# The conditional stage's fetches on SyncE in another order: expert numbers and weights one tile ahead

## What is computed

```
x = x + attn(cond(x, itok_8))
x = x + ffn(cond2(x, itok_15))

def cond2(x, indices):                       # the part that matters here
    h = gelu(x @ fc1_w.T + fc1_b)            # 256 -> 1024
    shared = h @ fc2_w.T + fc2_b             # 1024 -> 192
    expert_x = h @ experts_w[indices].T + experts_b[indices]   # 1024 -> 64, one of 16 experts per sequence
    return concatenate([shared, expert_x])
```

## Time and profile before

| | us |
|---|---|
| median of 3 runs | 1197.22 (1196.6 to 1199.02) |
| the profiled execution | 1193.99 |
| its span, first to last instruction | 1192.2 |
| phase 2 in it, from the first fc1 matmul to the first matmul of phase 3 | 391.16 to 601.24 |
| PE busy over the span | 1126.9 (95%) |

### The profile page before, as it was taken

The page is one execution under the profiler, slowest core; times in us unless marked ns, Lnnn a source line. Parts: engine busy times, 40 slices in busy tenths (PEclk is TensorE's granted clock), DMA queues, the critical chain, the costliest instruction groups (busy, mean ns, idle before and its releaser), DMA issues.

```text
span 1192.2 us, 18922 instructions
## 1 busy us (share of the span) xinstructions
PE 1126.9 (95%) x6178; PEld 898.6 (75%) x6178; DVE 803.2 (67%) x1440; ACT 594.3 (50%) x989; POOL 218.9 (18%) x266
## 2 busy tenths in 40 slices
PE   4899999999997899999699999999999999999998
PEld 3567777777764688878588888888888888888886
DVE  2776767767765655656448886588755887658775
ACT  1356556555564334433246555465554565555653
POOL 2243333433434243345100000000000000000000
PEclk9999999999999999999899999999999999999999
DMA  3341111221131446553623453134431344313430
GB/s 101 117 149 55 50 60 54 62 61 50 60 142 55 169 156 218 200 175 114 238 71 103 147 170 130 53 123 142 158 124 53 123 142 165 116 53 121 150 99 36
DMA packets 66763, 135.96 MB, mean 114 GB/s; under 512 B 13792, under 2 KB 28016, under 8 KB 66544
## 3 DMA queue, kind: packets, MB, share of 16 engines
q1 hardware_dynamic: 57696, 114.49, 29.4%
q10 hardware_dynamic: 9024, 20.97, 4.9%
HBM read 107.65 MB, written 30.41 MB: 116 GB/s over the span
## 4 chain that ended last, share of the span: by engine, by line
PE 75%; DVE 7%; SPq 6%; DMA 4%; POOL 4%; issue 3%; ACT 1%; DVEq 0%; POOLq 0%; ACTq 0%
PE bank L1459 34%; PE bank L1421 10%; PE bank L1471 5%; PE bank L1398 4%; PE bank L1209 3%; SPq L361 3%; PE bank L1190 3%; DVE neg_max L849 2%; PE bank L1267 2%; PE bank L1230 2%; PE bank L1193 2%; PE bank L1172 2%; DMA exp_raw<-in_exp_w 2%; POOL fc2b_lo L543 2%; PE bank L1156 2%
## 5 line engine op out<-in xcount | busy, mean ns | idle before, releaser
L1459 PE MATMUL bank<-op_lo,w_ring 128*128 128x512 f32 x896 | 348.6, 389 | 0.0
L1459 PE MATMUL bank<-op_hi,w_ring 128*128 128x512 f32 x896 | 348.6, 389 | 0.0
L1024 DVE TENSOR_TENSOR op_lo<-x_blk,op_hi 128x512 fp32r<-128x512 f32 x288 | 193.8, 684 | 30.4 <-ACT op_hi L722 30.3
L722 ACT ACTIVATE op_hi<-x_blk 128x512 fp32r<-128x512 f32 x288 | 162.8, 620 | 73.6 <-PE bank L1459 69.3
L1459 PEld LDWEIGHTS bank<-op_hi,w_ring 128*128 128x128 f32 x896 | 168.2, 188 | 34.9
L1459 PEld LDWEIGHTS bank<-op_lo,w_ring 128*128 128x128 f32 x896 | 168.2, 188 | 34.9
L849 DVE TENSOR_REDUCE neg_max<-bank 128x2 f32<-128x512 f32 (+1 forms) x192 | 126.0, 685 | 53.4 <-PE bank L1193 52.5
L576 ACT ACTIVATE p<-bank 128x512 f32<-128x512 f32 x192 | 111.2, 598 | 68.7 <-PE bank L1209 65.0
L746 ACT ACTIVATE x_blk<-x_blk,scales 128x512 f32<-128x512 f32 x96 | 69.3, 722 | 67.0 <-DVE x_blk L1077 28.9
L1421 PE MATMUL bank<-tile_hi,ffn_w 128*128 128x512 f32 x256 | 101.5, 396 | 0.0
L1421 PE MATMUL bank<-tile_lo,ffn_w 128*128 128x512 f32 x256 | 101.5, 396 | 0.0
(11 more groups left out here) (128 smaller groups left out, 1949.2 us busy)
## 6 DMA issues: line engine op xcount, KB each, us to landing
w_ring<-hid_scratch SPq DMA_DIRECT2D x112, 512.0 KB, 4.6
hid_scratch<-comb ACTq DMA_DIRECT2D x8, 1792.0 KB, 6.7
comb<-in_hid_d ACTq DMA_DIRECT2D x6, 768.0 KB, 4.6
xt<-in_x_t SPq DMA_DIRECT2D x16, 256.0 KB
xtok<-in_x_tok SPq DMA_DIRECT2D x16, 256.0 KB
resid<-in_x_t SPq DMA_DIRECT2D x16, 256.0 KB, 3.1
x_scratch<-x SPq DMA_DIRECT2D x16, 256.0 KB, 2.6
tile_in<-x_scratch SPq DMA_DIRECT2D x8, 512.0 KB, 4.2
```

The source lines that it names most:

```text
L722: nc.scalar.activation(op_hi[:, o % OP_RING, k], x_blk[:, operand_home(o), k], ACT.Copy).then_inc(s["op_hi"], 1)
L1024: nc.vector.tensor_tensor(op_lo[:, o % OP_RING, k], x_blk[:, operand_home(o), k], op_hi[:, o % OP_RING, k].bitcast(F32), ALU.subtract).the ...
L1459: last = mm(banks[first_bank + m][:, :], w, read(v[:, q % OP_RING, k, :]), start=k == 0 and v is op_hi and i not in (P2, P3), stop=k == KB ...
```

## The change

SP's program of the stage is written out for all tiles instead of looped, and put in another order. `load_expert` is divided: `expert_ids(t)` loads both numbers, `load_expert(t, ids)` issues both weight DMAs behind `expert_split` alone, and `load_expert_bias(t, ids)` issues both bias DMAs behind `y_ready`. In the round of tile t SP issues the input of tile t+1, the numbers and weights of t+1, the store of y of t, and the biases of t+1. The `w_ring` loads come behind everything that tile 7 needs, `load_y(1)` now stands ahead of the last store of `y`, and DVE has one added wait on `y_stored` in phase 3.

```diff
-            def load_expert(t):
-                for j in range(BT):
-                    e = sp.value_load(expert[0:1, bass.ds(t * BT + j, 1)], min_val=0, max_val=E - 1)
+            def expert_ids(t):
+                return [sp.value_load(expert[0:1, t * BT + j:t * BT + j + 1], min_val=0, max_val=E - 1) for j in range(BT)]
+
+            def load_expert(t, ids):
+                if t:
+                    sp.wait_ge(s["expert_split"], HEAD + BT * t)
+                for j, e in enumerate(ids):
                     sp.dma_start(exp_raw[:, j], exp_w[bass.ds(e, 1)].rearrange("a p k h -> p (a k) h")).then_inc(s["expert_loaded"], 16)
+
+            def load_expert_bias(t, ids):
+                if t:
+                    sp.wait_ge(s["y_ready"], HEAD + (1 + BT) * t)
+                    settle(sp, "sp_settled")
+                for j, e in enumerate(ids):
                     sp.dma_start(fc2_bias[SHARED - P:P, 1 + j:2 + j], exp_b[bass.ds(e, 1)].rearrange("a p o -> p (a o)")).then_inc(s["bias_loaded"], 16)
 
+            ids = expert_ids(0)
+            load_expert(0, ids)
             sp.dma_start(fc2_bias[:, 0:1], fc2_b[0]).then_inc(s["bias_loaded"], 16)
...
+            load_expert_bias(0, ids)
...
-            def cond2_tile(t, more):
-                if not is_first(t):
-                    sp.wait_ge(s["expert_split"], HEAD + BT * t)
-                    sp.wait_ge(s["y_ready"], HEAD + (1 + BT) * t)
-                    settle(sp, "sp_settled")
-                load_expert(t)
-                if more:
-                    load_x(t + 1)
-                else:
-                    sp.wait_ge(s["xa_split"], HEAD + TILES)
-                    sp.wait_ge(s["y_stored"], HEAD + 16)
-                    sp.dma_start(yc[:, :, :], y_scratch[:, :, 0:TW]).then_inc(s["yc_loaded"], 16)
+            def store_y(t):
                 sp.wait_ge(s["y_ready"], HEAD + (1 + BT) * (t + 1))
...
-            with sp.Fori(0, TILES - 1) as t:
-                cond2_tile(t, True)
...
+            for t in range(TILES - 1):
+                load_x(t + 1)
+                ids = expert_ids(t + 1)
+                load_expert(t + 1, ids)
+                store_y(t)
+                load_expert_bias(t + 1, ids)
+            sp.wait_ge(s["xa_split"], HEAD + TILES)
+            sp.wait_ge(s["y_stored"], HEAD + 16)
+            sp.dma_start(yc[:, :, :], y_scratch[:, :, 0:TW]).then_inc(s["yc_loaded"], 16)
             sp.wait_ge(s["comb_stored"], 16 * CHUNKS)
...
                 load_w(0, j)
-            cond2_tile(TILES - 1, False)
             load_y(1)
+            store_y(TILES - 1)
...
+                if pair == 0:
+                    dve.wait_ge(s["y_stored"], HEAD + 16 * TILES)
```

More of the change, by code:

```diff
@@ L367, in _ @@
                 sp.dma_start(fc2_bias[0:SHARED - P, 1 + j:2 + j], fc2_b[1, 0:SHARED - P]).then_inc(s["bias_loaded"], 16)
+            load_expert_bias(0, ids)
             def load_x(t):
                 sp.wait_ge(s["xa_split"], HEAD + t)
-                sp.dma_start(xa[:, :, :], x1_scratch[:, :, bass.ds(t * TW, TW)]).then_inc(s["xa_loaded"], 16)
-            def cond2_tile(t, more):
-                if not is_first(t):
-                    sp.wait_ge(s["expert_split"], HEAD + BT * t)
-                    sp.wait_ge(s["y_ready"], HEAD + (1 + BT) * t)
-                    settle(sp, "sp_settled")
-                load_expert(t)
-                if more:
-                    load_x(t + 1)
-                else:
-                    sp.wait_ge(s["xa_split"], HEAD + TILES)
-                    sp.wait_ge(s["y_stored"], HEAD + 16)
-                    sp.dma_start(yc[:, :, :], y_scratch[:, :, 0:TW]).then_inc(s["yc_loaded"], 16)
+                sp.dma_start(xa[:, :, :], x1_scratch[:, :, t * TW:(t + 1) * TW]).then_inc(s["xa_loaded"], 16)
+            def store_y(t):
                 sp.wait_ge(s["y_ready"], HEAD + (1 + BT) * (t + 1))
-                sp.dma_start(y_scratch[:, :, bass.ds(t * TW, TW)], y[:, :, :]).then_inc(s["y_stored"], 16)
-            with sp.Fori(0, TILES - 1) as t:
-                cond2_tile(t, True)
+                sp.dma_start(y_scratch[:, :, t * TW:(t + 1) * TW], y[:, :, :]).then_inc(s["y_stored"], 16)
             def load_y(t):
```

## The result

| | before | after |
|---|---|---|
| median, us | 1196.91 (1193.92 to 1199.02, 4 runs) | 1178.42 (1177.35 to 1179.79, 4 runs) |
| profiled execution, us | 1193.99 | 1179.1 |
| its span, us | 1192.2 | 1177.3 |
| phase 2 in it, us | 210.08 | 194.72 |
| phase 3 in it, us | 590.96 | 590.85 |

The ratio is 0.9848, with a 95% interval of 0.9824 to 0.9872: 1.5% less time, clear of the noise, but a small gain, under 2%. A second set of runs of the same two kernels gave 1180.6 against 1197.03, ratio 0.9869 (0.9832 to 0.9906).

A forecast was written before the change was run, and what follows sets the result against it. Phase 3 was bound by PE, phase 2 by a ring through SP's weight loads. Tile 1's start at 425.5 + 6 x 22.95 + 22.4 = 585.6 against 601.24, 15.6 us less: 1181.6, range 1173 to 1190.5.

The forecast's parts named there:

- The ring at SP, cut: Phase 2: weights issued a tile ahead, by about T + 12, landing by T + 15.5, before POOL wants them.
- the cover of 7 us: Phase 2: weights land by about T + 15.5, POOL wants them past T + 22; only lateness beyond that shows.
- Turns of POOL and DVE: Steady tiles of phase 2: DVE operations beside POOL's take 1.55 us each, last slice T + 16.3, tile 22.95 us.
- the full adding up: Rival, phase 2: POOL and DVE times add in full, a pair costs 3.64, 3.1 us more, 1200.3; chance 0.04.
- Tile 0: First tile of phase 2: a loss, POOL's eight operations slow DVE, tile 1 starts at 425.5 instead of 421.45.
- Tile 7: Last tile of phase 2: weights already there and no combine, so 22.4 us instead of 34.38.
- At nothing: Later w_ring loads, the written-out loop and DVE's new wait are covered; phase 3 stays at 591 us.
- The sum: Phase 2 ends at 585.6 against 601.24, 15.6 us less; profiled execution 1178.4, median 1181.6.
- The order did what it says: Against a rival in phase 2: weights still come last because SP's loads or waits end late, 1197.2; chance 0.03.
- A fallen clock: Rival, phase 2: PE's small waits in fc2a lower the clock, tiles of 24.5, 6.3 us less, 1190.9; chance 0.12.
- Turns that cost nothing: Rival, phase 2: turns cost nothing on the path, tiles of 22.2, 24.2 us less, 1173.0; chance 0.12.

The follow-up runs named there:

- both single-part experiments: Changed kernel with only tile 7's weight DMAs put back: 1188.41 us; kernel before with only tile 7's numbers, weights and first y load moved ahead: 1186.3 us.
- the variants with longer gaps: Changed kernel edited: weight DMAs behind the store of y, 1197.67 us; POOL's four combine operations made twice, 1210.28 us.

## Why the prediction was right, point by point

**The ring at SP, cut.** Right. POOL waits for PE, the weights are issued together at T + 11 (I had put T + 12), their DMAs take 2.5 to 3.0 us to land, and the cover of 7 us was there.

**Turns of POOL and DVE.** Right, and closest of all: the last slice was forecast at T + 16.3 and came at 16.3, the tile at 22.95 and measured 23.02. The runs turned this from an argument into something shown: taking the turns away gave 22.10, doubling `combine` gave 27.5 to 28.8, and moving POOL's start into the slices made tiles 1 to 6 longer than in the old order. A cast grew from 0.42 to 1.51, and a cast and a subtraction beside two POOL operations of 1.29 took 3.13 (451.99 to 455.12), not the full sum of 3.64. The rule in SBUF — State Buffer, section "Who interferes with whom", of the Trainium skill is that the engine that comes second to the shared ports blocks for the whole instruction of the first. The trace agrees with it in kind, and not with the full adding up that I had worked out for it; the measured 3.13 decides.

**Tile 0.** The mechanism was right, shown by the wait that took it away, and the size too: tile 1 was forecast to begin 4.05 us later after tile 0's start, and tile 0 grew by 3.8. POOL started at 404.51, 12.8 us into the tile, 0.4 later than put, and `fc2b` took 7.4 us as put. The closeness is in part luck: in the five other profiles in which POOL's part of tile 0 is that of the changed kernel, the tile took 33.5 to 35.25 us.

**Tile 7.** 22.4 forecast, 22.46 measured; both single-part experiments put it at 9 to 11 us.

**At nothing.** Phase 3 took 590.85 against 590.96. The new wait on DVE and the `w_ring` loads cost nothing that shows.

**The sum.** Forecast for phase 2: 15.6 us. Measured: 15.4. For the profiled execution: 1178.4, measured 1179.1. The median was forecast at 1181.6 and came at 1178.42, 3.2 us lower. The mis-sized term is the last one: I carried the 3.2 us between the profiled execution of before and its median over to the changed kernel, whose profile stands 0.7 us above its median. The 3.2 us were the place of one execution among those of the kernel before, which spread over 10 us. The changed kernel's have a narrower spread, so nothing says that its profile would stand as far below its median.

**Rivals.** The order did what it says: the weights' DMA came last only in tile 0. A fallen clock did not appear in tiles 1 to 7 of the changed kernel, but it did in the variants with longer gaps. Turns that cost nothing were wrong in the changed kernel and true once `combine` was moved.

## What to carry to other kernels

When a wait for a transfer is removed, look at what the waiting engine does next and beside whom: here POOL's four `combine` operations, begun 4, 11 or 13 us into a tile, went with tiles of 23.0, 25.3 to 26.8, and 22.1 us (in the second of these the split began 6 us later too). A transfer that a stage's last tile needs should be issued ahead of a bulk prefetch for the next stage; that alone was worth about 10 us here, the larger part of the gain. And an engine that is not the bottleneck can be held back on purpose, at the time when its neighbour on the path is done, as long as the work that is held back isn't itself what a later stage of the chain waits for, as it was when the weights came behind `y`.

## What the runs showed of the hardware that I had not expected

Two DMAs of 256 KB issued right behind seven of 512 KB by the same engine took 9.6 and 10.8 us to land, against 3.37 us for such a DMA in a middle tile of the kernel before. The same two DMAs, issued 2 and 3 us behind a store of 1.8 MB that another engine had issued, took 7.5 and 6.8 us, against 3.5 us each without it.

DVE and POOL went one for one where both had operations ready: in tile 2 six operations of DVE stood beside six of POOL and began 1.54 to 1.59 us apart, though DVE's take 0.42 and 0.69 us alone and POOL's 1.29.

One run of the old order in tiles 1 to 6 showed tiles of 22.5 and 28.1 us with the same work, the long ones with a granted clock of 0.94. A ring that leaves PE a gap is sensitive twice: the gap itself, and the lower clock of the work behind it.
